# Retention attention with ternary weights: the next block's operand halves made at other places of the hand-written order

## What is computed

```
xn  = layernorm(x)
h   = rmsnorm(xn) * qkv_norm_w
q, k, v = h @ ternary(qkv_w).T                  # per head, per chunk of 128 tokens
scores  = (q k^T) * mask                        # mask: exp(-s * (t - t')) under the diagonal
o   = scale * (scores v + (q * lam_t) S)        # S: the state carried from chunk to chunk
S   = lam_T * S + (k * lam_rev)^T v
s   = rmsnorm(rmsnorm(o) * norm_w) * proj_norm_w @ ternary(proj_w).T
g   = silu(xn @ ternary(ffn_w).T * scale + bias)
out = x + s * g
```

## Time and profile before

| | |
|---|---|
| Time, median of 3 runs | 1438.32 us (1437.77 to 1438.88) |
| Profiled execution | 1439.31 us, span of the profile 1437.9 us |
| Granted TensorE clock, mean | 0.995 |
| PE busy | 1388.2 us, 97% |
| DVE, ACT, POOL busy | 682.9 (47%), 413.3 (29%), 509.3 us (35%) |
| DMA | 74.66 MB, 52 GB/s on the mean |

### The profile page before, as it was taken

How to read it: one execution, slowest core, us unless ns; L and a number is a source line. 1 busy time by engine, 2 the same in 40 slices (tenths; PEclk the granted TensorE clock), 3 DMA queues, 4 the chain that set the end, 5 groups by cost and what they waited for, 6 DMA issues and landing times.

```text
span 1437.9 us, 26990 instructions
## 1 busy us (share of the span) xinstructions
PE 1388.2 (97%) x11537; PEld 953.8 (66%) x11537; DVE 682.9 (47%) x1183; ACT 413.3 (29%) x724; POOL 509.3 (35%) x492
## 2 busy tenths in 40 slices
PE   5999989999999999999999999999999999999998
PEld 2677667676665767667666676767657576676765
DVE  7884261734527155361634527255271543616324
ACT  6892131222213123131222313222131221312311
POOL 1523242434314352353322524353242423534331
PEclk9999999999999999999999999999999999999999
DMA  9420101002010020101102020020100201021000
GB/s 366 191 89 30 64 19 68 15 30 67 25 68 5 30 67 31 63 5 45 52 30 64 19 74 9 30 67 31 63 5 31 67 31 63 5 73 24 16 16 30
DMA packets 27769, 74.66 MB, mean 52 GB/s; under 512 B 6913, under 2 KB 10753, under 8 KB 27650
## 3 DMA queue, kind: packets, MB, share of 16 engines
q1 hardware_dynamic: 27360, 72.92, 15.1%
q10 hardware_dynamic: 290, 0.02, 0.0%
HBM read 56.12 MB, written 16.81 MB: 51 GB/s over the span
## 4 chain that ended last, share of the span: by engine, by line
PE 85%; DVE 8%; ACT 3%; issue 3%; DMA 1%; SPq 0%; ACTq 0%; DVEq 0%
PE ring L453 31%; PE ring L568 15%; PE ring L465 15%; PE ring L439 11%; PE att_ps L487 4%; DVE b_lo L829 2%; PE att_ps L531 2%; PE att_ps L527 2%; DVE o_lo L927 1%; ACT o_hi L1219 1%; DVE y_odd L789 1%; PE att_ps L509 1%; DVE arena L878 1%; PE ring L495 1%; DMA raw<-in_ffn_w 1%
## 5 line engine op out<-in xcount | busy, mean ns | idle before, releaser
L453 PE MATMUL ring<-b_hi,qkv_q 128*128 128x256 f16 x2048 | 451.2, 273 | 0.0
L453 PE MATMUL ring<-b_lo,qkv_q 128*128 128x256 f16 x2048 | 451.2, 273 | 0.0
L453 PEld LDWEIGHTS ring<-b_hi,qkv_q 128*128 128x128 fp8e4 x2048 | 201.6, 98 | 27.8
L453 PEld LDWEIGHTS ring<-b_lo,qkv_q 128*128 128x128 fp8e4 x2048 | 200.3, 98 | 28.0
L568 PE MATMUL ring<-proj_q,o_hi 128*128 128x512 fp8e4 x496 | 191.9, 387 | 26.2 <-DVE o_lo L927 26.2
L465 PE MATMUL ring<-qkv_q,b_hi 128*128 128x512 fp8e4 x512 | 194.2, 379 | 0.0
L465 PE MATMUL ring<-qkv_q,b_lo 128*128 128x512 fp8e4 x512 | 194.0, 379 | 0.0
L568 PE MATMUL ring<-proj_q,o_lo 128*128 128x512 fp8e4 x496 | 191.5, 386 | 0.0
L439 PE MATMUL ring<-ffn_q,a_hi 128*128 128x512 fp8e4 x480 | 183.7, 383 | 0.0
L439 PE MATMUL ring<-ffn_q,a_lo 128*128 128x512 fp8e4 x480 | 183.4, 382 | 0.0
L866 DVE TENSOR_TENSOR arena<-att_ps,mask 128x512 f32<-128x512 f32 x128 | 79.4, 682 | 159.1 <-PE att_ps L487 159.0
(11 more groups left out here) (156 smaller groups left out, 1889.6 us busy)
## 6 DMA issues: line engine op xcount, KB each, us to landing
xt<-in_x SPq DMA_DIRECT2D x32, 512.0 KB, 3.4
out<-xt SPq DMA_DIRECT2D x31, 512.0 KB, 2.6
raw<-in_qkv_w SPq DMA_DIRECT2D x24, 512.0 KB, 15.7
y<-in_x_turned SPq DMA_DIRECT2D x14, 512.0 KB, 4.3
y_odd<-in_x_turned SPq DMA_DIRECT2D x14, 512.0 KB, 5.5
raw<-in_ffn_w SPq DMA_DIRECT2D x8, 512.0 KB, 9.8
norm_rows<-norm_out SPq DMA_DIRECT2D x28, 128.0 KB, 4.2
raw<-in_proj_w SPq DMA_DIRECT2D x6, 512.0 KB, 4.8
```

The lines of the kernel that those rows point to most:

```text
L453: ins = pe.matmul(ring[:, b, e * BT:(e + 1) * BT], qkv_q[:, cb, o:o + P], part[:, cb, :], start=(cb == 0 and part is b_hi), stop=(cb == NC ...
```

## The change

- DVE: `split_a` of a block (both chunks, four L814) leaves the `attention` of the block before and stands at the head of the block itself, ahead of `output_scale(i - 1, 1)`. On ACT `high_a` goes the same way, ahead of `qk_out`.
- DVE: `centre(i + 1, 0)` leaves the middle of chunk 0's attention and stands ahead of the block's attention, behind the last `gate_out` of the block before. `norm_stats(i + 1, 0)` (and POOL's `norm_scale(i + 1, 0)`) go between the two `gate_out` (`add_out`) before it.
- DVE: `split_b(i + 1, 0, ·)` and `centre(i + 1, 1)` leave the middle of chunk 1's attention and stand at the end of chunk 0's, behind `add_state`. `split_b(i + 1, 1, ·)` stands around `split_o(i, 0)`. On ACT `high_b` of a chunk stands at the head of the attention.
- SP: the transposed x of block i + 1 is loaded at the head of block i, ahead of the stores; each `spread_norm` follows a store and the load behind it.
- PE: `scores` waits for the state only ahead of its second half.
- Block 0: `normalise(1, 1, again=True)` moves from chunk 1 to the end of chunk 0.

No instruction of arithmetic is added or removed. The diff:

```diff
@@ tensor
-                    pe.wait_ge(s_st, 2 * passes_on(g))
                 for half in range(HALF):
+                    if g > 0 and half == 1:
+                        pe.wait_ge(s_st, 2 * passes_on(g))
@@ vector, attention
-                if c == 1 and i == 0:
-                    normalise(1, 1, again=True)
...
-                if more and i > 0 and c == 1:
-                    split_b(i + 1, 0, 0)
-                    split_b(i + 1, 0, 1)
-                if more and i > 0:
-                    centre(i + 1, c)
...
                     elif more:
-                        split_a(i + 1, 1, 0)
+                        split_b(i + 1, 1, 0)
                     split_o(i, 0)
                     if i == 0:
                         take_b(1, 1, 1)
-                    elif more:
-                        split_a(i + 1, 1, 1)
+                        split_b(1, 1, 0)
                     if more:
-                        split_b(i + 1, 1, 0)
                         split_b(i + 1, 1, 1)
...
                         if i == 0:
                             take_b(1, 0, half)
-                            split_b(1, 0, half)
-                        elif more:
-                            split_a(i + 1, 0, half)
+                            if half == 0:
+                                normalise(1, 1, again=True)
+                        if more:
+                            split_b(i + 1, 0, half)
+                    if more and i > 0:
+                        centre(i + 1, 1)
@@ vector, blocks
+                if i > 1:
+                    for c in range(CHUNKS):
+                        split_a(i, c, 0)
+                        split_a(i, c, 1)
...
                     gate_out(i - 1, 1, 0)
+                    if i + 1 < NB:
+                        norm_stats(i + 1, 0)
                     gate_out(i - 1, 1, 1)
-                if 0 < i < NB - 1:
-                    norm_stats(i + 1, 0)
+                    if i + 1 < NB:
+                        centre(i + 1, 0)
@@ scalar, attention
+                if more and i > 0:
+                    high_b(i + 1, c, 0)
+                    high_b(i + 1, c, 1)
                 if i > 0:
                     silu(i, c, 0)
...
-                    if more and i > 0:
-                        high_a(i + 1, 1, 0)
                     high_o(i, 0)
@@ scalar, blocks
+                if i > 1:
+                    for c in range(CHUNKS):
+                        high_a(i, c, 0)
+                        high_a(i, c, 1)
@@ gpsimd, blocks
                     add_out(i - 1, 1, 0)
+                    if i + 1 < NB:
+                        norm_scale(i + 1, 0)
                     add_out(i - 1, 1, 1)
@@ sync
+                if i + 1 < NB:
                     for c in range(CHUNKS):
                         load_turned(i + 1, c)
-                    for c in range(CHUNKS):
+                for c in range(CHUNKS):
+                    store(i - 1, c)
+                    if i + 1 < NB:
                         spread_norm(i + 1, c)
```

More of the change, by code:

```diff
@@ L1228, in attention @@
                 if c == 1:
-                    if more and i > 0:
-                        high_a(i + 1, 1, 0)
                     high_o(i, 0)
[L1232 to L1236, removed]
+                    if i == 0:
+                        high_b(1, 1, 0)
+                        high_b(1, 1, 1)
                 square_o(i, c, 0)
@@ L1243, in attention @@
                     for half in range(HALF):
[L1244 to L1247, removed]
+                        if i == 0:
+                            high_b(1, 0, half)
                         if i > 1 or (i, half) == (1, 1):
@@ L1459, in gpsimd_program @@
                     decay_q(i, 0, 1)
-                if 0 < i < NB - 1:
-                    norm_scale(i + 1, 0)
                 attention(i, 0)
@@ L1531, in sync_program @@
                 load_weights(kind, t)
[L1532 to L1535, removed]
+            for i in range(1, NB):
+                if i + 1 < NB:
                     for c in range(CHUNKS):
                         load_turned(i + 1, c)
-                    for c in range(CHUNKS):
+                for c in range(CHUNKS):
+                    store(i - 1, c)
+                    if i + 1 < NB:
                         spread_norm(i + 1, c)
-                store(i, 0)
-            store(NB - 1, 1)
+            for c in range(CHUNKS):
+                store(NB - 1, c)
             for k in range(2):
```

## The result

| | before | after |
|---|---|---|
| Median of the runs | 1438.42 us (1437.77 to 1438.88, 4 runs) | 1450.01 us (1446.81 to 1456.12, 4 runs) |
| Span and granted clock of the profiled execution | 1437.9 us, 0.995 | 1454.9 us, 0.986 |

The changed kernel is slower: ratio 1.0086, 95% interval 1.0052 to 1.012. Forecast were 1446, slower, and a range of 1410 to 1455. What also changed is the scatter: four runs of after differ by 9.3 us, four of before by 1.1.

The account below looks back on a forecast made before the run. PE, busy 97%, bounds the kernel through its waits and clock. Terms -14.5 - 4.9 - 3.2 + 27.0 + 8.2 - 3.6 - 0.8 = +8.2 us on 1439.3 gave 1447.5, forecast as a 1446 median, range 1410 to 1455.

Parts of the forecast that it names:

- Ten stalls at `project_out`, -14.5: PE's 1.48 us wait for `o_lo` in ten ordinary blocks goes, ten times 1.45 us saved.
- blocks 3, 7, 11, -4.9: PE's 2.14 us wait for `o_lo` in these blocks falls to block 15's 0.52, saving 3 x 1.62 us.
- That is a new stall of 2.7 us: PE waits for L851 before ffn half 1 in ten blocks, as L830 and `centre` take turns with POOL: +27.0 us.
- Rivals one and two: One: POOL doesn't hold DVE's queue up, 1411, chance 0.28; two: two short DVE instructions pass per POOL's one, 1433, 0.15.
- Between none of ten and all ten I take five: 5 x 1.65 = +8.2: PE's clock falls behind five of the ten new stalls, 1.65 us each; range 0 to 16.5 us.
- Block 1, -3.6: The 4.46 us wait becomes three pieces of 1 to 2 us, -0.9, and the clock's fall, 2.7, may go.
- `spread_gamma` about 1: In block 1, `spread_gamma` waits about 1 us, needing the decay of DVE and POOL behind the late mask.
- The fall of the clock ... may go: In block 1, the clock's fall behind the old 4.46 us wait, worth 2.7 us, may disappear.
- Block 0, -0.8: `normalise(1, 1)` no longer stands between the mask and `output_scale`, shortening PE's wait by 0.8 us.
- The state's wait, 0: Waiting for the state only in the second half of `scores` gains nothing beyond block 0's -0.8.
- - 3.2: The clock no longer falls behind the `project_out` waits of blocks 7 and 11, two times 1.6 us saved.
- - 2.7: Block 1's clock part: its fall, 2.7 us in ten-odd slowed products, may go.

Follow-up runs that it names:

- the first experiment: The changed kernel with the eight L830 moved behind `norm_stats` in chunk 0, ahead of the second `ffn_bias`; 1413.95 us, ratio 0.9829.

## Why the prediction was right, step by step

- *Ten stalls at `project_out`, -14.5, and blocks 3, 7, 11, -4.9: right.* L569 waits 1.0 us in block 1 and 0.5 in each of 3, 7, 11 and 15, and nowhere else. The four L830 ahead of `o_lo` cost nothing: it is 0.39 us early.
- *"That is a new stall of 2.7 us", +27.0: right*, measured 26.3 in ten, at the ten blocks named, and for the reason given. Moved away, or beside short partners, it is gone, and a longer queue of POOL makes it longer. Rivals one and two fall with this: DVE was held up, and, but for the seventh L830, by one instruction of POOL for each of its own.
- *"Between none of ten and all ten I take five: 5 x 1.65 = +8.2": the term that was mis-sized.* The size of one fall, 1.7 us, was right, their number was not. The profiled execution has eleven lengths of it behind nine of ten waits, the median run (13.0 - 1.7 for block 1) / 1.7, about seven, and the quickest (8.7 - 1.7) / 1.7 = four (estimates, if block 1 lost the same in each). It isn't a number that the program sets: it differs from run to run of one kernel. Filling the wait gave 10.0 us back.
- *Block 1, -3.6: only in part.* The pieces came as said (1.86 and 0.96; the third, "`spread_gamma` about 1", did not come: its wait fell into the first). "The fall of the clock ... may go" was too good: it halved, since 1.86 us is still followed by one. The DMA of `centre` landed at 186.8, not at 188.4: it was issued at 182.85, 2.4 us earlier than before, where I had allowed for 1, and flew 4.0 us (4.2 assumed). And it was not the only bound: the L830, which I had not held up in this block, ended at 186.76.
- *Block 0, -0.8:* -0.57. *The state's wait, 0:* 0, as run.
- *The sum.* Terms without clock: -14.5 - 4.9 + 27.0 - 0.9 - 0.8 = +5.9, measured +5.0. Terms of clock: +8.2 - 3.2 - 2.7 = +2.3, measured +5.8 in the median run and +13.2 in the profiled one (12.0 without what lies inside the waits). Together +8.2 forecast, +11.6 measured. The clock came out 3.5 higher than forecast and the waiting 0.9 lower (0.8 is the looseness of the split), so the direction was right by its cause, and the size fell as near as it did with some luck: the profiled execution alone is 17 us above before's.

What the Trainium skill says in SBUF — State Buffer, "Who interferes with whom", is that these two engines contend for an exclusive lock, held for the whole instruction. The trace agrees: the L830 taken up at 268.10 ends at 270.60, 0.14 us behind an L1380 of 2.35 us. What comes next when both wait, which the page doesn't say, is shown here for these instructions.

Two things stay open. L1449 stood for 10.56 us beside L703 running back to back, where here two queues took turns. One more row of DVE in the kernel before says how long it stood still:

```profile
72.93 1.99 DVE L731 TENSOR_SCALAR cols<-cols,peak 128x8 f32<-128x8 f32 x1
```

The last L703 is through at 73.01. Behind it this L731 of eight columns takes 1.99 us and ends at 74.92, with L1449 (74.90). So by this row L1449 got no turn for 8.7 us, as long as one L703 followed another, and then did its work in 1.9. Yet the same L703 took its turn beside L1349, so the difference lies with POOL's operation or with which engine's queue was running first, and no run tried which. And the waits of blocks 6 and 4 are alike, 2.62 and 2.63 us, with a fall behind the one of block 4 and none behind block 6: which waits of this length the clock answers was counted, not explained.

## What to carry to other kernels

Before work is moved into an engine's idle time, look at what its partner on the same memory does in that time: a short instruction that has to take turns costs the length of the partner's, so eight of 0.27 us can take nine. Put many short ones where the partner waits or has short ones too. And price a wait of a busy TensorE twice, once as waiting and once as clock, with the second as a range that runs of one kernel differ in.

## What the runs showed of the hardware that I had not expected

- The alternation held while POOL's instructions followed one another with less than 0.1 us between them: L830, with two inputs in SBUF, had 0.35 us alone and 1.13, 1.20, 2.05, 2.50 beside instructions of POOL of about 1.1, 1.0, 1.89 and 2.35, one each. A gap of 0.14 us on POOL was enough for one to slip through. The mask, which has one input in PSUM, was not held: in the first experiment its four took the usual 2.48 us beside POOL's two sums (271.28 to 273.76, the sums 269.97 to 274.54).
- More work made the kernel quicker: 200 useless transposes, 22 us of PE, took 10.0 us off 1450.0 and brought the scatter from 9.3 to 1.4 us.
- A clock of 0.979 on the mean of a whole run, 31 us, came nearly all from waits of 4.0 us in ten places, each of which by itself looks like a quarter of a per cent. 6.8 of the 31 us lay inside the waits and cost nothing, so span x (1 - clock) overstates the loss.
